# Gathering the rows of each super-tile of edges once, in two edge stages of a two-layer graph network

## The reference, cut to what matters

```python
dst = jnp.minimum((6250 * jax.random.uniform(...) ** 2.0).astype(jnp.int32), 49999)
_o = jnp.argsort(dst, stable=True)
...
key_e = k_rel[edge_type, edge_src]
val_e = v_rel[edge_type, edge_src]
att = (q[edge_dst] * key_e).sum(-1) * rel_pri[edge_type] / jnp.sqrt(jnp.float32(dk))
...
hsum = jax.ops.segment_sum(w[:, :, None] * val_e, seg, num_segments=S)
...
e = jax.nn.leaky_relu(a_src[src] + a_dst[dst], NEG_SLOPE)
...
msg = x[src] * alpha[:, :, None]
out = jax.ops.segment_sum(msg, dst, num_segments=n)
```

## Time and profile before

| what | us |
|---|---|
| timed runs, median of 3 (lowest to highest) | 4169.86 (4167.93 to 4179.78) |
| profiled execution: span, first to last instruction | 4487.9 |
| first gather stage, 569 to 1912 | 1343 |
| stage of sums, 2087 to 2608 | 521 |
| second gather stage, 2987 to 4317 | 1330 |

### The profile page before, as it was taken

One profiled execution on the slowest core, in us unless ns is written; L12 is line 12 of the kernel. 1 busy time (PEld: TensorE's weight loads), 2 busy tenths in 40 slices (PEclk: granted clock), 3 DMA queues, 4 the chain that ended last, 5 costly groups with the idle time before them and its releaser, 6 DMA issues. The chain is left out here.

```text
span 4487.9 us, 50605 instructions
## 1 busy us (share of the span) xinstructions
PE 2636.7 (59%) x10364; PEld 1802.2 (40%) x10365; DVE 2869.6 (64%) x5456; ACT 1640.2 (37%) x4268; POOL 2419.6 (54%) x2361
## 2 busy tenths in 40 slices
PE   0499845555656565612888867734555546555553
PEld 0255423333333333302666655523444434443442
DVE  4544434578777877895888866634555555555557
ACT  2244322333433433341444435422333333333343
POOL 4322266677677667701444444446666666666651
PEclk9999967766676766655999989966776777777776
DMA  6366698888888888804777721134555555555552
GB/s 202 126 257 256 266 288 267 260 265 262 258 261 267 252 266 262 258 24 141 234 238 234 237 63 35 33 70 138 161 168 162 168 159 166 167 160 167 162 150 92
DMA packets 607757, 852.98 MB, mean 190 GB/s; under 512 B 158649, under 2 KB 501445, under 8 KB 600987
## 3 DMA queue, kind: packets, MB, share of 16 engines
q0 software_dynamic: 128272, 451.36, 32.6%
q1 hardware_dynamic: 466614, 386.90, 27.4%
q10 hardware_dynamic: 12686, 12.72, 0.9%
HBM read 560.70 MB, written 291.24 MB: 190 GB/s over the span
## 5 line engine op out<-in xcount | busy, mean ns | idle before, releaser
L1051 POOL DMA_INDIRECT rows<-kv,kvi x880 | 930.8, 1058 | 425.8 <-issue 256.4
L2224 POOL DMA_INDIRECT g_rows<-x1t,srci x880 | 842.1, 957 | 474.8 <-issue 240.6
L1127 PE MATMUL psD<-qs,hot 128*128 x1760 | 695.3, 535 | 497.5 <-issue 263.2
L1127 PEld LDWEIGHTS psD<-qs,hot 128*128 128x128 f32 x1760 | 418.8, 263 | 727.6 <-issue 671.0
L2378 PE MATMUL g_psM<-g_rows,g_hot 128*128 128x264 f32 x1760 | 622.4, 513 | 63.7 <-issue 31.8
L1339 DVE TENSOR_TENSOR prod<-rows,psD 128x512 f32<-128x512 f32 x440 | 300.2, 682 | 390.9 <-DMA hsort<-hrow,tposi 197.5
L2378 PEld LDWEIGHTS g_psM<-g_rows,g_hot 128*128 128x128 f32 x1760 | 423.6, 253 | 177.1 <-issue 76.8
L1211 ACT ACTIVATE off<-psB,npiota 128x256 f32<-128x256 f32 x440 | 206.7, 470 | 746.2 <-DMA hsort<-hrow,tposi 294.0
L1715 PE MATMUL psM<-wv,vhot 128*128 128x260 f32 x1760 | 430.7, 393 | 82.0 <-ACT wv L1664 58.5
L1715 PEld LDWEIGHTS psM<-wv,vhot 128*128 128x128 f32 x1760 | 322.7, 191 | 189.9 <-issue 81.4
L1634 POOL TENSOR_TENSOR wv<-vrows,wgt 128x1024 f32<-128x1024 f32 x110 | 231.8, 2107 | 285.7 <-DVE vhot L1743 210.8
(11 more groups left out here) (447 smaller groups left out, 4446.2 us busy)
## 6 DMA issues: line engine op xcount, KB each, us to landing
val_v<-rows SPq DMA_DIRECT2D x220, 512.0 KB
vrows<-val_v SPq DMA_DIRECT2D x220, 512.0 KB
sums_v<-g_run SPq DMA_DIRECT2D x110, 528.0 KB
g_drow<-drow_v SPq DMA_DIRECT2D x55, 512.0 KB
rows<-kv,kvi POOLq DMA_INDIRECT x880
g_rows<-x1t,srci POOLq DMA_INDIRECT x880
xs<-in_x ACTq DMA_DIRECT2D x12, 896.0 KB, 10.3
g_ndt<-nodeb SPq DMA_DIRECT2D x440, 6.0 KB
```

The lines of the kernel that those rows point to most:

```text
L1051: nc.gpsimd.indirect_dma_start(out=rows[:, k], out_offset=None, in_=table, in_offset=bass.IndirectOffsetOnAxis(ap=index[:, i * SLOTS + k:i ...
L1127: nc.tensor.matmul(psD[:, 2 * (V % 2) + j, 0:D], hot[:, V % 2, j * P:(j + 1) * P], node[:, ds(blk[V % 4], 1)].rearrange("p o d -> p (o d)" ...
L2224: nc.gpsimd.indirect_dma_start(out=rows[:, i % NBUF, k, 0:ROW1], out_offset=None, in_=dr["x1t"], in_offset=bass.IndirectOffsetOnAxis(ap=v[ ...
```

## The change

Both gather stages gather every super-tile once: 784 gathers instead of 880 in each. The visits find their rows by a register that holds the seat of their super-tile in a ring.

In `prepare_edges`, `kvi` and `srci` are laid out by super-tile (784 columns). New tables are computed on DVE in the time between two steps: for each visit its seat in the ring (`seat_e`, and `turns` for layer 1) and the number of groups that have to be there (`need_e`), and for each super-tile the number of visits that must be over before it may be overwritten (`past_e`, and `turns`). Records have four fields instead of six. There are still 440 visits.

In the first gather stage the ring has eight super-tiles, as before 16 slots. SP counts the groups that have arrived (`arrived`) and those that are free again (`freed`, two groups behind, when `prod_done` has reached a number that it loads into a register). DVE loads four seats and four needs per four visits. The transfers of flags and scores move from SP's queue to ACT's. The value rows are stored by super-tile, so 196 stores of 512 KB instead of 220. The lag of the softmax pieces, `LAG`, goes from 2 to 3.

The stage of sums loads the value rows by visit, 440 transfers of 256 KB, at an address from a register.

In the second gather stage the ring has 24 super-tiles, 48 slots, refilled in groups of four super-tiles (eight gathers) when the visits that need them have been weighted (`wv_done`). POOL counts arrivals itself: after the third gather of a group it waits for the group before. The weighted rows go to a buffer of their own (`wv`), two tiles at a time, and ACT copies the source scores of a chunk's eight visits into a small tile (`es`) from which DVE reads them.

```diff
+RE = 8
+RA = 24
+BA = 4
+CV = 8
+TURNS = NV + NS // BA + NV // CV
...
-STEPS, LAG = 43, 2
+STEPS, LAG = 43, 3
+NG = NS // 2
+GE = RE // 2
...
-                for i in range(NI):
-                    for g in range(SLOTS // GS):
-                        if i:
-                            pool.wait_ge(prod_done, (i - 1) * (SLOTS // 2) + (g + 1) * (GS // 2))
-                            pool.wait_ge(kept[g], 16 * i)
-                        for k in range(g * GS, (g + 1) * GS):
...
+                for n in range(NG):
+                    i, g = divmod(n, GE)
+                    if i:
+                        pool.wait_ge(freed, n - GE + 1)
+                        pool.wait_ge(kept[g], 16 * i)
+                    for k in range(GS):
+                        nc.gpsimd.indirect_dma_start(
+                            out=rows[:, g * GS + k], out_offset=None, in_=table,
+                            in_offset=bass.IndirectOffsetOnAxis(ap=index[:, n * GS + k:n * GS + k + 1], axis=0)).then_inc(got[g * GS + k], 16)
...
-                for n in range(NTICK):
-                    i, g = divmod(n, SLOTS // GS)
+                for n in range(NG):
+                    i, g = divmod(n, GE)
                     for k in range(g * GS, (g + 1) * GS):
                         sp.wait_ge(got[k], 16 * (i + 1))
+                    sp.sem_inc(arrived, 1)
                     o = dr["val"].rearrange("(i k p) d -> i p k d", k=GS, p=P)[n]
                     sp.dma_start(o, rows[:, g * GS:(g + 1) * GS, D:2 * D]).then_inc(kept[g], 16)
...
+                    m = n - 2
+                    if 0 <= m < NG - GE:
+                        if m % 4 == 0:
+                            past = nc.values_load_multi_w_load_instructions(v["past_e"][0:1, m:m + 4], engines=[mybir.EngineType.SP], min_val=1, max_val=NV)[1]
+                        sp.wait_ge(prod_done, past[m % 4])
+                        sp.sem_inc(freed, 1)
...
                 def pair(V):
-                    i, k = divmod(2 * V, SLOTS)
                     b = 2 * (V % 2)
-                    dve.wait_ge(got[k], 16 * (i + 1))
-                    dve.wait_ge(got[k + 1], 16 * (i + 1))
+                    if V % 4 == 0:
+                        dve.load(seats, v["seat_e"][0:1, V:V + 4])
+                        needs = nc.values_load_multi_w_load_instructions(v["need_e"][0:1, V:V + 4], engines=[mybir.EngineType.DVE], min_val=1, max_val=NG)[1]
...
+                    dve.wait_ge(arrived, need_of[V % 4])
                     dve.wait_ge(dst_done, 2 * V + 2)
...
-                    tt(prod[:, b:b + 2], rows[:, k:k + 2, 0:D], psD[:, b:b + 2, 0:D], ALU.mult).then_inc(prod_done, 1)
+                    tt(prod[:, b:b + 2], rows[:, ds(seat_of[V % 4], 2), 0:D], psD[:, b:b + 2, 0:D], ALU.mult).then_inc(prod_done, 1)
...
-                        o = dr["val"].rearrange("(i k p) d -> i p k d", k=GS, p=P)[ds(i * NG + g, 1)]
-                        sp.dma_start(rows[:, g * GS:(g + 1) * GS], o.rearrange("o p k d -> (o p) k d")).then_inc(loaded[g], 16)
+                        for u in range(2):
...
+                            k = g * GS + 2 * u
+                            sp.dma_start(rows[:, k:k + 2], values[ds(at, 1)].rearrange("o p k d -> (o p) k d")).then_inc(loaded[g], 16)
...
-                        if i >= NBUF:
-                            pool.wait_ge(sum_done, CV * (i - NBUF) + 2 * g + 2)
...
+                def landed(m):
+                    pool.wait_ge(got[m % RM], 32 * BA * (m // RM + 1))
+                    pool.sem_inc(arrived, 1)
+                for m in range(NM):
+                    f = m - RM
+                    if f >= 0:
+                        if f % 4 == 0:
...
+                            past = nc.values_load_multi_w_load_instructions(turns[0:1, NV + f:NV + f + 4], engines=[mybir.EngineType.Pool], min_val=1, max_val=NV)[1]
+                        pool.wait_ge(wv_done, past[f % 4])
+                        pool.sem_inc(reused, 1)
+                    for k in range(2 * BA):
...
+                        if k == 2 and m:
+                            landed(m - 1)
+                landed(NM - 1)
...
+                def source_scores(i):
+                    last = act.value_load(turns[0:1, NV + NS // BA + i:NV + NS // BA + i + 1], min_val=1, max_val=NS // BA)
+                    for u in range(CV):
+                        if u % 4 == 0:
+                            act.load(regs, turns[0:1, CV * i + u:CV * i + u + 4])
+                            seat = [act.snap(r, min_val=0, max_val=2 * RA - 2) for r in regs]
+                        if u == 0:
+                            act.wait_ge(arrived, last)
+                        ins = nc.scalar.copy(es[:, i % 2, 2 * u:2 * u + 2], rows[:, ds(seat[u % 4], 2), D:ROW1])
+                    ins.then_inc(es_done, 1)
...
-                    tt(out, out, w.unsqueeze(3).to_broadcast([P, GRP, H, DK]), ALU.mult).then_inc(wv_done, 1)
...
+                    for u in range(2):
+                        k = g * GRP + 2 * u
+                        mine = rows[:, ds(seat[2 * (g % 2) + u], 2), 0:D].rearrange("p k (h d) -> p k h d", h=H)
...
+                        tt(wv[:, i % 2, k:k + 2, 0:D].rearrange("p k (h d) -> p k h d", h=H), mine,
+                           w.unsqueeze(3).to_broadcast([P, 2, H, DK]), ALU.mult).then_inc(wv_done, 1)
```

195 lines of the change are left out of this document (129 added, 66 removed).

## The result

The changed kernel takes 4149.40 us (median of 5 runs, 4145.37 to 4160.67), the kernel before 4171.47 us beside it (5 runs, 4167.93 to 4182.14). The ratio is 0.9948, with a 95% interval of 0.9931 to 0.9965: 0.5% faster, where 3.5% was forecast. 4149 lies in the range, at its far end.

A forecast was written before the change was run, and what follows sets the result against it. POOL's gather queue was taken as the bound, with DVE at its limit in most of the first stage afterwards. Rest 1815 + first stage 1142 + second 1026 + unplaced 44 = 4027, stated as 4025 us; range 3920 to 4165.

The forecast's parts named there:

- What bounds the kernel: Both gather stages: POOL's gather queue sets the time, 1.255 us per gather, 880 gathers or 1104 us each.
- The 44 us: Whole kernel: median of timed runs, 4169.9 us, over the summed floor of 4126; added unplaced to the forecast.
- Fewer gathers: Both gather stages: 96 fewer gathers each save 120 us of POOL per stage, the gain lying late in each.
- New work on DVE: Later part of first gather stage: register loads and small register instructions leave 31 us uncovered, ends 0 and 88.
- The new hand-over: First gather stage: waits for groups counted and freed through SP cost 0 on average, up to 98 us without slack.
- The slack of 0.6 us: First gather stage: SP's hand-over takes 5.7 us, POOL needs 6.3 us to be ready, so the difference hides it.
- The landed wait: Second gather stage: group counts as arrived after three gathers of the next; 10 us with ring release, between 0 and 69.
- The chain of the second stage: Last third of second gather stage: chain takes 17.6 us per chunk against POOL's 16.1, adding 25 us.
- The long gathers: First gather stage: gathers longer than the median add 96 us of POOL, kept unchanged; 83 if proportional to gathers.
- POOL stays the only bound: Rival, whole kernel: register loads fully covered, DVE above 0.95, chain without stalls; 3930 us, chance 0.15.
- The new hand-over takes the gain back: Rival: first stage stays at 1200 us, total 4085; with one gather's stall per chunk in the second, 4144; chance 0.17.
- The slower chain: Rival, second gather stage: the carry chain is the bound and lengthens; 4327 us, or about 4220 if half; chance 0.13.

The follow-up runs named there:

- second profile: The kernel before, unchanged, run and profiled again: 4171.44 us, profiled span 4169.7 us.
- constant seats: The changed kernel, but DVE in the first gather stage takes seats and numbers of groups as constants, without register work: 4047.79 us.
- one number on DVE: The changed kernel with DVE loading one number of groups per four visits, not four, and the second stage's wait for landings four gathers later: 4038.89 us.

## Why the prediction was wrong

**What bounds the kernel: right.** POOL's 0.949 + 0.30 us per gather was the floor of both stages. The 44 us that the sum did not place are found in the second profile: the gathers of the first stage take 1219 us and not 1200 (15 of these 19 us are the gathers' own time, 946.0 against 930.8; the rest are short waits), those of the second 1114.6 and not 1111, 6 and 24.5 us follow behind the last gathers, and the remaining stages are 10 shorter.

**Fewer gathers: right.** 120 us in the second stage were forecast; left out alone, the gathers gave 1139.1 - 1020.4 = 119. In the first stage POOL is the bound for the first fifth (222 us; 221 for 90 visits), and for the rest DVE is at 0.93 where 0.94 was taken, with POOL about as full. Without the price of the machinery the sum has (221 + 835 / 0.94) + 991 + (1815 + 44) = 3959 us, and 3959.4 was measured. That it fits so well is luck: these parts, first stage, second stage and all else, measured 1129 (for 1109), 1020 (for 991) and 1810 (for 1859). The second was too low because no term stood for what follows behind the last gather (24 us), and the 44 us that were added to the whole hid both.

**New work on DVE: the step that failed.** It took 31 us, one load per four visits, with ends 0 and 88; the runs show 97. The step counted loads and let the rest go at nothing: "2 loads of registers and small register instructions". The second list of the order shows the rest, a line of eight small instructions behind the second load, and no row of before has a price for them; they should have had two ends like the others. At 186 and 23 ns each they are 836 ns per four visits, more than the two loads together. The argument that DVE's last instruction still works meanwhile holds at times only: from nothing to all of the 2.3 us is covered, and the idle time in front of every fourth product of the later part adds up to 108 us, 85 more than with constant seats. The Trainium skill (Runtime: NRT & Kernel Launch, "Instruction fetch mechanics") has about 200 ns for each register that is loaded. The rows here have 345 ns for four, so its price does not hold here, and the 176 us by it are 79 above the 97, where the 31 are 66 below. What is paid per register here is the check.

**The new hand-over: too low.** Taken at 0, because POOL waits for DVE anyway after the first 90 visits; measured 29 us, with what else is new in the stage. 17 of them lie in the first fifth, which the argument had left out, and 14 in the second; 15 are won back by freeing a group sooner, so these are the hand-over's. The slack of 0.6 us between 5.7 and 6.3 us was read from one hand-over at the end of the stage; in the first fifth of the changed kernel SP's store comes 5.3 us after the last gather at the median, but up to 8.0.

**The landed wait: too low, for a reason in plain sight.** "I add 10 us, between 0 and one gather per chunk (55 x 1.255 = 69)"; measured 73.2 us of waits and 57 us of the stage. The bound was put in chunks, but the wait comes once per group, 97 times, and the price is what a landing takes beyond three gathers. The hand-over of the earlier trace rows was at hand: 5.3 us from the last gather's start to the store, more than 4 x 1.25 = 5.0 us from there to the fourth gather of the next group.

**The chain of the second stage: no cost.** 25 us were added; POOL waited 3.0 us for the weighting, and 7.3 with the landed wait moved. (The 25 rest on 106 super-tiles in the last 132 visits. The list `TWICE` has 23 of its numbers there, so it is 109, and the same sum gives 17.) That the second stage came to 1026.3 us with the wait moved, the number that the prediction had for it, is chance: 991 + 10 + 25 there, gathers and their tail here.

The prediction put 31 / 0.94 + 10 + 25 = 68 us on the machinery of both stages. The stages show 97 + 29 + 57 + 6 = 189, and the timed difference between the change and the gathers merely left out is 190 (the two profiled spans are 199 apart, 10 of them outside these stages). That is the whole error: 3959 + 68 = 4027.

**The long gathers** were kept at 96 us as belonging to the stage. The change has 838.3 - 784 x 0.946 = 97, but the second profile of before 946.0 - 880 x 0.949 = 111, which would go with the number of gathers (111 x 784 / 880 = 99). But the first profile of before has 96 for the same 880, so two executions of one kernel differ by as much, and no rule follows. The Trainium skill (SBUF — State Buffer, "SBUF: two separate sides") would tie them to DVE's own steps; these are the same in both kernels, and these sums neither show nor exclude it. The sentence that the sum would be 13 us lower does not follow either: the first stage was added up as 221 + 921, from DVE, and the long gathers stand only in POOL's floor and in the rival of 3930.

**The rivals.** "POOL stays the only bound" did not come: in the later part POOL waits 159.3 us for SP, and even with the gathers merely left out that part took 907 us, not 859. "The new hand-over takes the gain back", with a stall per chunk in the second stage as well, had the time (4144) nearly right. Its stall in the second stage did come (57 us, for 59), but its 58 us of hand-over in the first are at most 29; the 97 us of the registers are no part of it. So 86 of the 189 us are its own, and the time is chance. The slower chain did not come, and its rows are from an execution that was not like the timed runs.

## What to carry to other kernels

Here a saving on one queue was paid for on the queues that had to find the data. So price every instruction of the lookup, the checks of loaded values too, on the engine that becomes the bound once the saving is made, and put it on one that has room (here PE: the same four checked numbers, 20 us better than one number on DVE). A wait that an issuing engine makes for its own transfers is priced by the landing time against the work issued in between, once per group; putting it four gathers later was a change of one digit and worth 60 us. And to learn what a change can bring at all, run the saving without its machinery: one run parted 211 us of gain from 190 us of price.

## What the runs showed of the hardware that was not expected

A register value whose bounds are asserted costs 186 + 23 ns of DVE's queue, and a load of four registers 345 ns, so the checks of four values cost more than two loads of four. At times a load takes far longer: 33 of the 110 loads of seats took over 0.6 us, one 1347 ns; what they wait for is open. DVE's queue runs ahead of the engine by more than one instruction, so that 2.3 us of register work can vanish; behind a product it does not: the reduction, which otherwise starts before the product has ended, came up to 2.4 us late. The stage of sums took 511 us before and 522 with the change, for the same bytes, with DVE, PE and POOL as busy in both. It is not the price of its smaller transfers: of the ten other kernels with the same code of that stage, seven take 487 to 490 us from the first to the last product of its sums, as before did (489), and three take 496 to 501, as the change did (498). They differ in other stages alone; why the stage differs was not settled.
